# The second context asked for behind the first keys, the constants ahead of the first context

## The reference

```python
x = x + _L0_xattn_ref(_layernorm(x), ctx_1024, Wq, bq, Wkv, bkv, Wout, bout)
...
q = query @ Wq + bq
kv = context @ Wkv + bkv            # 16 heads of 16
scores = einsum('bhid,bhjd->bhij', q, k) * SCALE
attn = softmax(scores)
out = einsum('bhij,bhjd->bhid', attn, v) @ Wout + bout
```

## Time and profile before

| | us |
|---|---|
| median of 3 runs (lowest, highest) | 1431.11 (1430.5, 1432.84) |
| profiled execution, its own time | 1430.48 |
| its span | 1428.7 |

### The profile page before, as it was taken

How to read it: one execution, slowest core, us unless ns; L and a number is a source line. 1 busy time by engine, 2 the same in 40 slices (tenths; PEclk the granted TensorE clock), 3 DMA queues, 4 the chain that set the end, 5 groups by cost and what they waited for, 6 DMA issues and landing times. The chain is left out here.

```text
span 1428.7 us, 33786 instructions
## 1 busy us (share of the span) xinstructions
PE 1299.7 (91%) x14368; PEld 1145.5 (80%) x14368; DVE 733.6 (51%) x1149; ACT 600.3 (42%) x958; POOL 514.7 (36%) x505
## 2 busy tenths in 40 slices
PE   5799999999999999999999878677999999877689
PEld 4789998999898989989998667345888888766578
DVE  5565466557555764665573427445223233564632
ACT  4555555555555555555555122334433333211300
POOL 4643233234323432332341005623654544254400
PEclk9999999999999999999999559997999999989989
DMA  6855764757475657656563202003110100014035
GB/s 187 192 138 124 162 146 117 150 123 167 99 179 132 144 118 167 141 126 142 127 141 77 64 22 90 1 0 119 43 52 32 62 11 0 0 30 174 1 139 205
DMA packets 51618, 148.05 MB, mean 104 GB/s; under 512 B 23752, under 2 KB 28184, under 8 KB 49432
## 3 DMA queue, kind: packets, MB, share of 16 engines
q1 hardware_dynamic: 50328, 144.99, 40.8%
q10 hardware_dynamic: 1152, 1.05, 0.2%
HBM read 62.29 MB, written 1.31 MB: 45 GB/s over the span
## 5 line engine op out<-in xcount | busy, mean ns | idle before, releaser
L366 ACT ACTIVATE xa_pt<-xa_sc 128x1024 f32<-128x1024 f32 (+1 forms) x224 | 212.6, 964 | 149.6 <-PE xa_sc L558 149.6
L412 DVE TENSOR_REDUCE xa_mx<-xa_sc 128x2 f32<-128x804 f32 x256 | 243.5, 992 | 41.2 <-PE xa_sc L542 40.9
L558 PE MATMUL xa_sc<-xa_queries,xa_keys 104*128 104x128 f32 (+1 forms) x1664 | 232.3, 285 | 2.2 <-DVE xa_queries L427 1.8
L558 PEld LDWEIGHTS xa_sc<-xa_queries,xa_keys 104*128 104x128 f32 (+1 forms) x1664 | 206.5, 195 | 20.9 <-issue 8.1
L1153 PE MATMUL moe_GU<-moe_lnH,moe_gu 128*128 128x512 f32 (+1 forms) x480 | 154.8, 401 | 6.8 <-DVE moe_h L1301 4.4
L479 PE MATMUL xa_pj<-xa_ctx_hi,xa_wk 128*128 128x400 f32 (+1 forms) x512 | 156.9, 348 | 0.9 <-DVE xa_qst L440 0.9
L479 PE MATMUL xa_pj<-xa_wv,xa_ctx_hi 128*128 128x256 f32 (+1 forms) x832 | 155.3, 286 | 0.1
L542 PE MATMUL xa_sc<-xa_keys,xa_queries 96*128 96x402 f32 x512 | 137.7, 371 | 13.3 <-DMA xa_keys<-xa_kst_hi 7.6
L300 POOL TENSOR_TENSOR xa_kst_lo<-xa_wk,xa_kst_hi 128x400 fp32r<-128x400 f32 x64 | 67.3, 1052 | 226.3 <-ACT xa_kst_hi L345 226.3
L569 PE MATMUL xa_op<-xa_pt,xa_values 128*32 128x64 f32 x6656 | 141.1, 228 | 7.7 <-ACT xa_pt L366 3.3
L295 POOL TENSOR_TENSOR xa_ctx_lo<-xa_raw,xa_ctx_hi 128x1600 fp32r<-128x1600 f32 (+1 forms) x32 | 116.0, 3625 | 78.0 <-DVE xa_ctx_hi L405 75.3
(11 more groups left out here) (244 smaller groups left out, 2041.6 us busy)
## 6 DMA issues: line engine op xcount, KB each, us to landing
xa_keys<-xa_kst_hi SPq DMA_DIRECT2D x256, 200.2 KB, 6.0
xa_keys<-xa_kst_lo SPq DMA_DIRECT2D x128, 200.2 KB, 5.2
xa_raw<-in_ctxT SPq DMA_DIRECT2D x15, 1601.0 KB, 8.8
gf_w<-in_gf_w SPq DMA_DIRECT2D x16, 1024.0 KB, 7.2
moe_gu_raw<-in_moe_gu SPq DMA_DIRECT2D x10, 704.0 KB, 4.1
moe_dn_raw<-in_moe_down SPq DMA_DIRECT2D x10, 384.0 KB, 3.1
xa_queries<-xa_qst SPq DMA_DIRECT2D x96, 32.0 KB, 3.4
X<-in_x SPq DMA_DIRECT2D x1, 1024.0 KB, 5.8
```

Source lines behind the costliest of these rows:

```text
L366: nc.scalar.activation(PT[ptslot(step)][0:rows, 0:nt], SC[bank(step)][0:rows, 0:nt], ACT.Exp, scale=float(D0) ** -0.5).then_inc(ex_done, 1)
L412: nc.vector.tensor_reduce(mx[:, u // 2, 2 * (u % 2):2 * (u % 2) + 2], SC[bank(step)][:, :, 0:MXN], AX.X, ALU.max).then_inc(mx_done, 1)
L558: last = mm(SC[bank(step)][0:rows, kk, a * P:(a + 1) * P], KS[:, 2 * a + h, kt * P:kt * P + rows], QS[b % 2][:, 2 * a + h, :], start=True, ...
```

## The change

The constants' transfer is issued in front of the first context's two pieces. The second context's transfer, with its two waits, and the four copies of rows of ones move on SyncE's queue from `cv 0` to behind the twelve key copies of the last block of `K 0 0`, and so behind the query copies too. Later contexts stay where they were. Nothing else in the program differs.

```diff
     sp.dma_start(X[:], w["x"].rearrange("(t p) n -> p t n", p=P)).then_inc(E["x_in"], 16)
     sp.dma_start(E["wk"][:], w["wk"]).then_inc(E["wk_in"], 16)
+    sp.dma_start(consts[:], w["consts"]).then_inc(E["consts_in"], 16)
     for (lo, hi), landed in zip(CVCOLS, (E["raw_half"], E["raw_in"])):
         sp.dma_start(E["raw"][:, :, lo:min(hi, NK)], ctxT[0][:, :, lo:min(hi, NK)]).then_inc(landed, 16)
-    sp.dma_start(consts[:], w["consts"]).then_inc(E["consts_in"], 16)
     sp.dma_start(E["wv"][:], w["wv"]).then_inc(E["wv_in"], 16)
...
+            def raw_load(b):
+
+                before = nth("cv", b - 1, 0, 1)
+                sp.wait_ge(csum_done, before * 2)
+                sp.wait_ge(lo_done, before)
+                sp.dma_start(raw[:, :, 0:NK], ctxT[b]).then_inc(raw_in, 16)
+
...
             for step in order:
                 k, b, h, u = step
-                if (k, u) == ("cv", 1) and b + 1 < B:
-
-                    sp.wait_ge(csum_done, nth(*step) * 2)
-                    sp.wait_ge(lo_done, nth(*step))
-                    sp.dma_start(raw[:, :, 0:NK], ctxT[b + 1]).then_inc(raw_in, 16)
-                    if b == 0:
-                        sp.wait_ge(rows_in, 16)
-                        for a in range(4):
-                            sp.dma_start(*constant_rows(o_sb, slice(96 + 2 * a, 98 + 2 * a), 2 * a, 2 * a + 2)).then_inc(rows_in, 16)
+                if (k, u) == ("cv", 1) and 0 < b < B - 1:
+                    raw_load(b + 1)
                 if step in (("K", 0, 0, 3), ("K", 0, 1, 3)):
                     keys(0, h)
+                if step == ("K", 0, 0, 3):
+                    raw_load(1)
+                    sp.wait_ge(rows_in, 16)
+                    for a in range(4):
+                        sp.dma_start(*constant_rows(o_sb, slice(96 + 2 * a, 98 + 2 * a), 2 * a, 2 * a + 2)).then_inc(rows_in, 16)
```

## The result

The changed kernel took 1442.07 us as the median of four runs (1441.71 to 1442.37), beside 1430.80 of the kernel before (1430.29 to 1432.84): a ratio of 1.0076, 95% interval 1.0058 to 1.0093. That is 11.3 us slower, where the forecast was 8.4 slower with a range up to 1443.5. Its profiled execution has a span of 1440.6 us, against 1428.7.

What follows compares the result with a forecast made beforehand. TensorE, busy 91% of the span, was taken to bound the kernel. Its shift of +8.4 us from the late context, plus 0 for the constants, took 1430.48 to 1438.9, or 1439.5 as median; range 1433.5 to 1443.5.

Steps and rivals of the forecast that it cites:

- Part 1: First batch's keys on SyncE: first copy issued at 31.6 instead of 35.60, last landing at 46.0, first hole 4.0 us shorter.
- Part 2: Second context issued at 40.4 instead of 25.42, landing at 51.0; batch 1's first value product 8.4 us later, at 67.5.
- L: Landing time of the second context, forecast 51.0 us, bounds 45.6 and 53.2.
- The chain behind L: Splits, low parts, bias additions, key low part and ScalarE's eviction, from context landing to batch 1's first value product: 16.5 us.
- Who ends last: Before batch 1's first value product, GpSimd's chain (67.5) ends after TensorE's own path (65.0, up to 66.9), by at least 0.6.
- side path: TensorE's own steps from the third score step (59.5) to the value product: 65.0, up to 66.9 at low clock.
- Part 3: Transfers moved along: ones copies cost nothing, second-half keys land near 63 with cover 12 us or more, third context near 69.
- Part 4: Constants ahead of the first context in the opening: nothing behind them moves, 0, bounds -0.3 and +0.4 us.
- the measuring point: Batch 1's first value product on TensorE, at 59.08 before; TensorE is gapless from there, so its shift is the kernel's.
- overtake the keys: Rival at the transfer queues: the second context passes most keys, sum +3.0 to +5, 1434 to 1436; chance 0.12.
- The earlier keys: Rival at the first hole: earlier keys win, late split hidden, 5.9 us gained, 1425.2; needs landing by 41.2; chance 0.07.
- slip free: Rival in the opening: VectorE's normalisations mostly finish before GpSimd starts, last transposes some 3 us sooner, +5, 1436.5; chance 0.05.

Runs made afterwards that it cites:

- the two parts alone: Two kernels: kernel before with only the constants moved ahead of the first context, ratio 0.9986; changed kernel with the constants put back, ratio 1.0059.
- the context alone: Changed kernel with the constants back behind the first context, so only the second context's move (with the ones copies): 1442.34 us, ratio 1.0059 to the kernel before.
- the last of the kernels above: Kernel before with ones copies behind the first twelve key copies, bias additions late, 18 unused products before the first score product: ratio 0.9984.
- The first kernel with filled holes: Changed kernel with late bias additions and unused products in TensorE's holes (17 before first score product, 33 before batch 1's first key product): ratio 1.0074.
- The kernel with the constants alone: Kernel before with only the constants' transfer moved ahead of the first context: ratio 0.9986 to the kernel before.

## Why the prediction was right, and where its sizes were off

- **What bounds, and where to read.** Right. TensorE's first value product of batch 1 was the right point: it moved by 10.46 us, and the first mark by 10.56.
- **Part 1, the keys.** The direction was right, the gain 2.4 us instead of 4.0: the last key at 47.6, not 46.0. The queries started at 28.1 and not 27.2 (the opening ran 0.4 to 0.9 us late by spread, as the two parts alone show), their issue took 3.90 instead of 4.42, and the keys took 15.6 us from the first issue to the last landing, not 14.4. That last term looks like more than spread: the five kernels with the context right behind the twelve copies have 15.1 to 15.6, the four with the order of before have 14.1 to 14.5. I had carried the 14.4 over unchanged, although the neighbours of the keys in the queue change, ahead of them and behind; which of the two costs the microsecond is not shown.
- **Part 2, the landing.** L was 53.0, where I said 51.0: the 1.6 us of the keys, and 5.4 us behind the last key where I had taken 5.0 from the earlier trace rows. The borrowed pattern was a good one, and the bound of 53.2 just held it. This is the term that was mis-sized, with 2.0 us.
- **The chain behind L.** I said L + 16.5; it was L + 16.57 here and L + 16.6 with the context alone. Each link is in the rows above: the second casts ended 0.9 us after GpSimd's part (58.59 against 57.67). One of them took 2.37 us beside it, the other 0.57 alone. The Trainium skill's page "SBUF — State Buffer", section "SBUF: two separate sides", has the shared port pair as an exclusive lock, for which the second of the two engines blocks fully; this trace agrees.
- **Who ends last.** Half right. I said that GpSimd's chain ends last by at least 0.6 us; it was by 0.45, since TensorE's own path took 7.75 us from the third score step (61.34 to 69.09) at the low clock, where I had allowed 7.4 (59.5 to 66.9). That it is no cause by itself, I had not seen: without the additions the distance is 16.4, with the clock held up too it is 14.6. The low clock was in my sum as a side path, and it is an equal partner.
- **Part 3.** Right: keys of the second half and the third context arrived in time; no wait for them shows in TensorE's gaps.
- **Part 4, the constants.** Right, 0, shown by its own run.
- **Behind the measuring point** I expected the same shift at every mark. It held up to 801 us (10.64), and then 1.3 us came in the pair of executions that was profiled. That stages far behind can add or take a microsecond or several I had not allowed for. How much of it is in the medians' 11.3 is not shown.
- **The bounds.** My worked high end was +10.6, from L = 53.2. The value product, at +10.46, stayed under it, with L only 0.2 us from its bound. The whole, +11.3 (+11.0 counted from the median I started from), passed it. The range held it only because it reached to +12.4, and I had named no term for the last 1.8 us. That much of the hit is room and not working.
- **The rivals.** The context does not overtake the keys (shown with the context ahead of the keys and after eight of them). The earlier keys did not win, for the reason given: L was 53.0, and not 41.2 or less. The opening did not slip free: ScalarE took up the first context at 10.52, just behind its square root as before.

## What to carry to other kernels

A transfer that lands early and waits unused is no waste if the chain behind it is long: before moving it back, write down the chain from its landing to the engine that bounds, and compare that with the wait which you want to shorten. Here keys that came 2.4 us sooner were paid for with a chain of 16.6 us laid open. Look for small transfers that cost the issuing queue time without being needed soon; moving these four copies of 25 KB brought 2 us at the mark, while the 1.6 MB ahead of them cost the queries' issue 0.07 us. And when two chains end within half a microsecond of each other, removing one shows nothing; remove both before you call either harmless.

## What the runs showed of the hardware that was not expected

**A short stop in TensorE's stream, and then a fall of the granted clock.** In the last of the kernels above the clock is low in a stretch without any idle time:

```profile
167.00:173.00 6.00, 6.00 (x95) 5.41 (x95) 1.29 (x3) 1.61 (x2) 0.00 (x0) 0.50 0.36 80
```

The stretch of the kernel before which answers to it has full clock:

```profile
170.00:176.00 6.00, 5.85 (x106) 5.48 (x107) 3.15 (x5) 3.09 (x5) 0.62 (x1) 1.00 0.64 146
```

But 2.4 us ahead of the fall, which came at 166.7, 32 products that stand in one row in the kernel before (at 166.68) are torn in two:

```profile
163.02 0.43 PE L572 MATMUL xa_op<-xa_pt,xa_values 128*32 128x64 f32 x16
164.31 0.43 PE L572 MATMUL xa_op<-xa_pt,xa_values 128*32 128x64 f32 x16 [0.86 <-issue]
```

"issue" means that the engine waited for nothing that the profile shows. The stop, and 6.8 us at half speed, which cost at most 3.4, cover the 3.8 us that were lost. The first kernel with filled holes lost 4.0 us between the marks 654 and 704 in the same way: a stop of 1.13 us that ends at 666.12, and a granted clock of 0.50 from about 667.3 to 674. From 72 to 784 us the fourteen traces show no other fall. A stop of 0.75 us (at 266) and five of 0.16 to 0.38 us had no fall behind them. So a stop that small can be followed by a fall, but need not be. What makes these stops is open. Three of the four kernels that have any carry products without use, which make TensorE's stream longer; whether that matters was not tried.

It means that a gain of 1 to 4 us in one stage has to be read at that stage's end, and not in one execution's whole time. The kernel with the constants alone is an example: its profiled execution is 0.24 us ahead of the kernel before at the first mark, and 3.1 us behind it at the end.

**Small copies slow the issue of the copies behind them.** Six query copies took 6.57, 6.38, 6.44 and 6.70 us in the four kernels with the context and the four copies of ones right ahead of them, 3.96 to 3.97 in the three with the context alone ahead, and 3.89 to 3.90 in the seven with nothing. So 2.6 us of the 6.6 go to the 25 KB copies, beside the 2.8 that these take to issue.
